# An edge-sorting graph kernel: the row numbers of its one-hots move to PSUM, its first steps and its plan are reordered

## What is computed

```
h        = relu(layernorm(x))                                   # x: 12500 x 256
in_deg   = min(segment_sum(1, dst), 511);  out_deg = min(segment_sum(1, src), 511)
sum3d    = segment_sum(edge_attr @ W_sum + b_sum, src)          # 212500 x 128 -> 12500 x 256
cent     = sigmoid(centralities @ W_cent + b_cent);  vor = sigmoid(voronoi @ W_vor + b_vor)
out      = x + h + z_in[in_deg] + z_out[out_deg] + cent + vor + sum3d
```

## Time and profile before

| what | value |
|---|---|
| times of three runs | 2588.72, 2579.75, 2586.4 us (median 2586.4) |
| the profiled execution's own time | 2585.49 us |
| its span in the profile | 2583.7 us |
| POOL busy | 1921.2 us, 74% of the span, 1869 instructions |
| DVE busy | 1754.8 us, 68% |
| PE busy | 1697.2 us, 66% |
| ACT busy | 764.1 us, 30% |
| DMA | 451.92 MB, 175 GB/s on average |

### The profile page before, as it was taken

One profiled execution on the slowest core, in us unless ns is written; L12 is line 12 of the kernel. 1 busy time (PEld: TensorE's weight loads), 2 busy tenths in 40 slices (PEclk: granted clock), 3 DMA queues, 4 the chain that ended last, 5 costly groups with the idle time before them and its releaser, 6 DMA issues. The chain is left out here.

```text
span 2583.7 us, 40662 instructions
## 1 busy us (share of the span) xinstructions
PE 1697.2 (66%) x8685; PEld 1207.0 (47%) x8685; DVE 1754.8 (68%) x5839; ACT 764.1 (30%) x3968; POOL 1921.2 (74%) x1869
## 2 busy tenths in 40 slices
PE   4755666655656565556877777674677785588766
PEld 1224444443334443334655555552565563476555
DVE  8764556778776587886766665552666674599776
ACT  1322222344442344444232323323233322001100
POOL 4877777777777777777777777777777777745787
PEclk7855665555556555557888888885889997899877
DMA  4336544445555443336776777774788785898975
GB/s 110 87 105 184 163 123 127 129 137 171 177 168 157 127 124 109 100 95 188 235 216 204 215 212 213 204 214 123 227 236 243 230 241 163 188 242 210 252 199 149
DMA packets 484919, 451.92 MB, mean 175 GB/s; under 512 B 72379, under 2 KB 444609, under 8 KB 484675
## 3 DMA queue, kind: packets, MB, share of 16 engines
q1 hardware_dynamic: 402782, 300.08, 43.3%
q0 software_dynamic: 78752, 136.44, 16.7%
q10 hardware_dynamic: 3140, 12.80, 1.5%
HBM read 319.28 MB, written 129.59 MB: 174 GB/s over the span
## 5 line engine op out<-in xcount | busy, mean ns | idle before, releaser
L476 POOL DMA_INDIRECT sorted<-edge_ring,pos_i x1660 | 1666.9, 1004 | 537.9 <-issue 483.5
L937 PE MATMUL bank<-piece_ring,hot_n 128*125 128x129 f32 x4920 | 901.0, 333 | 192.4 <-DVE hot_n L627 186.8
L937 PEld LDWEIGHTS bank<-piece_ring,hot_n 128*125 128x125 f32 x4920 | 776.6, 227 | 367.9 <-DVE hot_n L627 319.9
L627 DVE SCALAR_TENSOR_TENSOR hot_n<-bank,wkey,piece_ring 128x250 f32<-128x250 f32 x1230 | 576.7, 469 | 137.8 <-DMA piece_ring<-sorted 134.9
L825 ACT ACTIVATE junk<-bank,mark_col 128x100 bf16<-128x100 f32 x1664 | 548.5, 341 | 264.0 <-PE bank L921 263.4
L927 PE MATMUL bank<-hot_w,after_b 128*128 128x400 bf16 x416 | 183.1, 440 | 364.9 <-ACT junk L825 362.5
L832 ACT ACTIVATE edge_ring<-key_f 128x5 f32<-128x5 f32 x332 | 70.5, 212 | 1165.5 <-DMA edge_ring<-in_edge_attr_dram 1164.8
L961 PE MATMUL bank<-hot_dl,hot_dh 128*125 128x100 bf16 x1661 | 245.0, 303 | 235.4 <-DVE hot_dh L562 234.3
L652 DVE TENSOR_TENSOR acc<-bank,acc 125x129 f32 x1230 | 347.7, 283 | 51.1 <-PE bank L937 36.4
L763 DVE CAST pos_i<-pos_f 128x4 int32<-128x4 f32 x416 | 78.1, 188 | 444.9 <-ACT junk L825 441.0
L961 PEld LDWEIGHTS bank<-hot_dl,hot_dh 128*125 128x125 bf16 x1661 | 202.6, 207 | 310.9 <-DVE hot_dh L562 291.9
(11 more groups left out here) (99 smaller groups left out, 1081.4 us busy)
## 6 DMA issues: line engine op xcount, KB each, us to landing
piece_ring<-sorted SPq DMA_DIRECT2D x1230, 130.0 KB
edge_ring<-in_edge_attr_dram SPq DMA_DIRECT2D x332, 320.0 KB
sorted<-edge_ring,pos_i POOLq DMA_INDIRECT x1660
base<-in_x_dram SPq DMA_DIRECT2D x20, 560.0 KB
out_dram<-base ACTq DMA_DIRECT2D x20, 560.0 KB
out_dram<-base SPq DMA_DIRECT2D x9, 560.0 KB
base<-out_dram SPq DMA_DIRECT2D x9, 560.0 KB
edge_ring<-in_L_gnn_z_in_dram,deg_i POOLq DMA_INDIRECT x100, 6.6
```

What stands on the lines that cost most here:

```text
L476: g.indirect_dma_start(rows, bass.IndirectOffsetOnAxis(index, 0), edge_ring[:, slot, at, :], None).then_inc(s_scatter[slot], 16)
L627: v.scalar_tensor_tensor(out=hot_n[:, n % HOT_SLOTS, 0:G, :], in0=iota_ps.unsqueeze(1).to_broadcast([P, G, LOC]), scalar=wkey[:, s % 2, c: ...
L937: last = t_.matmul(to, hot_n[:, n % HOT_SLOTS, k, :], piece_ring[:, n % PIECE_SLOTS, k, 0:SUM], start=(k == 0), stop=(k == ROW_GROUPS[s] - 1))
```

## The change

- The row numbers for `hot_tiles` are now also in PSUM: `iota_h` is copied, as 125 f32 words, into a free part of bank 4 and read from there as bf16 pairs (`iota_pair`). All 1664 one-hots of the four kinds read them there instead of from SBUF.
- For the first two quads (`INDEX_FIRST`) `index(q)` stands ahead of the side work. The lists of segment 0 move from quad 0 to quad 8, the two further source key chunks from quads 0 and 1 to quads 3 and 6, and the totals of the next segment start ten quads into a segment instead of one.
- Segments are 40, 170, 125 and 81 quads. `HEAD` grows to 160 columns so that the first 40 quads have their keys from chunk 0. The pieces become 180, 440, 350 and 260.
- `acc` is zeroed by five ACT instructions over 2580 elements (a broadcast zero column) at quads 2, 6, 10, 14 and 18, instead of four DVE memsets. The first fold waits for all five.
- The planner's table of costs has other numbers, and its budget for a quad is 5.5 instead of 5.1.

```diff
-HEAD = 100
+HEAD = 160
-SEGMENT_QUADS = (25, 185, 125, 81)
+SEGMENT_QUADS = (40, 170, 125, 81)
+INDEX_FIRST = 2
-BUDGET = 5.1
+BUDGET = 5.5
-BASE = (0.7, 1.4, 2.5)
+BASE = (0.8, 1.4, 2.5)
...
-    CLEARS = 4
+    CLEARS = 5
...
-    put(0, ("lists", 0, 0))
+    put(8, ("lists", 0, 0))
     for i in range(CLEARS):
-        put(2 + 2 * i, ("clear", i, 0))
+        put(2 + 4 * i, ("clear", i, 0))
     for i in range(1, SRC_KEYS):
-        put(i - 1, ("keys", i, 0))
+        put(3 * i, ("keys", i, 0))
...
-        if left and q >= quad0[s] + 1:
+        if left and q >= quad0[s] + 10:
...
+        zero_col = sb("zero_col", [P, 1])
...
+        iota_pair = bank[4][:, P:P + LOC].bitcast(BF16).rearrange("p (n t) -> p n t", t=2)
...
             v.tensor_copy(iota_ps, iota_n[:, 0:LOC])
+            dve.wait_ge(s_made, 3)
+            link(v.tensor_copy(bank[4][:, P:P + LOC], iota_h[:, :, :].rearrange("p n t -> p (n t)").bitcast(F32)))
...
                 return v.tensor_tensor(to, part.unsqueeze(2).to_broadcast([P, 2, n, 2]),
-                                       iota_h[:, 0:n, :].unsqueeze(1).to_broadcast([P, 2, n, 2]), ALU.is_equal)
+                                       iota_pair[:, 0:n, :].unsqueeze(1).to_broadcast([P, 2, n, 2]), ALU.is_equal)
...
+                if n == 0:
+                    dve.wait_ge(s_acc_clear, CLEARS)
...
-            def clear(i):
-                n = SW // CLEARS
-                cleared[0] = mark(v.memset(acc[:, i * n:(i + 1) * n, :], 0.0))
...
                     hot_rows(q + 1)
+                if q < INDEX_FIRST:
+                    index(q)
...
-                index(q)
+                if q >= INDEX_FIRST:
+                    index(q)
...
+                    elif what == "clear":
+                        n = SW // CLEARS
+                        a.activation(acc[:, s * n:(s + 1) * n, :].rearrange("p w n -> p (w n)"),
+                                     zero_col[:, :].to_broadcast([P, n * SUM]), ACT.Copy).then_inc(s_acc_clear, 1)
```

More of the change, by code:

```diff
@@ L53 @@
 COUNTED = 2
-BUDGET = 5.1
+BUDGET = 5.5
 BACKLOG = 2.0
-BASE = (0.7, 1.4, 2.5)
-COST = {"keys": (8.0, 0.0, 0.0), "totals": (0.36, 0.4, 0.0), "starts": (2.0, 0.0, 0.0), "lists": (8.0, 2.0, 0.0),
-        "hist": (0.65, 1.1, 0.0), "stats": (0.62, 0.0, 0.0), "degrees": (2.0, 0.0, 0.0), "indegrees": (0.3, 0.0, 0.0),
-        "clear": (3.5, 0.0, 0.0), "node": (2.3, 0.0, 1.3), "piece2": (0.78, 0.75, 0.0)}
+BASE = (0.8, 1.4, 2.5)
+COST = {"keys": (8.0, 0.0, 0.0), "totals": (0.42, 0.43, 0.0), "starts": (2.0, 0.0, 0.0), "lists": (8.0, 2.0, 0.0),
+        "hist": (0.85, 1.1, 0.0), "stats": (0.62, 0.0, 0.0), "degrees": (2.0, 0.0, 0.0), "indegrees": (0.3, 0.0, 0.0),
+        "clear": (0.0, 0.0, 2.5), "node": (2.3, 0.0, 1.3), "piece2": (0.78, 0.75, 0.0)}
 def gnn_kernel(nc, x, src, dst, edge, cent, vor, z_in, z_out, w_cent, b_cent, w_vor, b_vor, w_sum, b_sum,
@@ L296, in gnn_kernel @@
         s_cleared = sem("s_cleared")
+        s_acc_clear = sem("s_acc_clear")
         s_keys = sem("s_keys")
@@ L518, in _ @@
             v.memset(mark_col[:, :], -MARK)
+            v.memset(zero_col[:, :], 0.0)
             v.memset(ones_b[:, :], 1.0).then_inc(s_cleared, 1)
@@ L646, in fold @@
                 dve.wait_ge(s_piece, n + 1)
-                if n == 0:
-                    need(cleared[0])
-                else:
+                if n > 0:
                     dve.wait_ge(s_summed, n)
@@ L652, in fold @@
                 v.tensor_tensor(to, ps_piece[n % PIECE_BANKS][0:LOC, 0:SUM], to, ALU.add).then_inc(s_summed, 1)
-            cleared = [0]
-            def clear(i):
-                n = SW // CLEARS
-                cleared[0] = mark(v.memset(acc[:, i * n:(i + 1) * n, :], 0.0))
             def hist(h):
@@ L765, in _ @@
             keys(0)
-            dve.wait_ge(s_made, 3)
             for h in range(quad0[1]):
@@ L789, in _ @@
                         degrees(s)
-                    elif what == "clear":
-                        clear(s)
                     elif what == "node":
```

## The result

The changed kernel takes 2523.5 us in the median (2522.8 to 2524.1, four runs) against 2587.6 us of the kernel before (2579.8 to 2589.3, four runs). The ratio is 0.976 with a 95% interval of 0.974 to 0.977. The prediction said 2524 us, with a range of its own of 2501 to 2550, and the measurement agrees. Its rivals A (2546), B (2642) and C (2568) did not come about.

What follows compares the result with a forecast made beforehand. POOL's chain of indirect-DMA scatters was taken to bound the kernel. Terms 5.4 + 2.0 + 11.0 + 43.5 = 61.9 us off the profiled 2585.5 gave 2523.6, with 0.9 to the median 2524 us, range 2501 to 2550.

Steps and rivals of the forecast that it cites:

- A: DVE's one-hots from PSUM run at the f32 rate, 170 us more DVE work, mostly absorbed: 2546 us; chance 0.12.
- B: PSUM one-hots at f32 rate and DVE's waits stay, POOL starves 118 us at quads 90 to 219: 2642 us; chance 0.07.
- C: Any DVE one-hot reading SBUF at the pair rate still holds POOL, so 43.5 us stay: 2568 us; chance 0.08.
- First scatter: POOL's start: quad 0's cast moves right behind the first one-hots, start at 27.9 us instead of 33.3, 5.4 us less.
- Second quad: POOL's wait of 2.31 us at 41.23 falls to 0.30, 2.0 us less, if the next quads come faster.
- One-hots: `hot_tiles` on DVE has one SBUF input, so scatters are held less: 43.5 us less, bounds 19.9 and 64.3.
- mean below 0.96 before 430 us: Sign of being right: POOL's scatters at line 476 have a mean duration below 0.96 us before 430 us.
- Memsets: Four memsets of 2746 ns leave DVE and no longer stretch POOL's scatters: 11.0 us less, bounds 9 to 13.
- DVE at the same rate: DVE instructions comparing with row numbers in PSUM keep 359 and 412 ns: cost taken as zero.
- What holds POOL: Some DVE instructions with two SBUF inputs stretch scatters, 1.24 us instead of 0.96; an input in PSUM seems the difference.
- Clears on ACT: Five zeroing instructions on ACT, 2.2 us each, at most 4.4, covered by keys and casts running ahead: cost nothing.
- Plan: Planner and segments spread the same instructions otherwise, no more or less POOL work: 0 us if DVE keeps ahead.

## Why the prediction was right, step by step

- **First scatter, 5.4 us**: measured 5.85 (33.26 to 27.41). The size of the added totals was right to half a microsecond.
- **Second quad, 2.0 us**: measured 2.01, the wait of 2.31 is the usual 0.30.
- **One-hots, 43.5 us**: the stretches say 11.3 us (165 to 430, predicted 13.3), 18.7 (430 to 1165, predicted 20.0) and 3.9 (1200 on, predicted 6.6). Taking the step back alone costs 47 us of time and 49.4 of durations, so it is a little larger than its term. By stretch it brings back 17.4 us of excess (19.4 less 2.0), 20.1 (38.5 less 18.4) and 8.8 (11.5 less 2.7): the split of the shared 37.1 us was right, and the stretches on either side of it were set too low. The sign "mean below 0.96 before 430 us" did not come: from 165 to 430 us it is 0.964 (201.57 / 209).
- **Memsets, 11.0 us**: the size was right and the cause was not. The first stretch lost 17.3 us of excess where 11.0 + 3.6 were predicted, and the four long scatters are gone, but ACT was not needed for it: with the memsets still on DVE, PSUM one-hots remove all four and the new order three. The step that failed is the sentence that charged the 3.4 us to the memset because it lay in the scatter; the instructions behind it were not looked at. That the sum came out in spite of it is luck: the three edits remove the same hold, and it was counted once.
- **DVE at the same rate, 0 us**: right, 354 and 406 ns. The rule of the Trainium skill that gave rivals A and B, one element a cycle for tensor_tensor with any operand in PSUM ("VectorE: DVE Perf Modes", "The perf-mode tier table"), does not hold for bf16 here. "At most two" ("Why PSUM operands drop a tier") fits both rates.
- **What holds POOL**: the earlier trace rows were read rightly. The page "SBUF — State Buffer" of the Trainium skill, section "SBUF: two separate sides", says that a DVE operation with two SBUF inputs, or in a two-port mode, and a GpSimd operation exclude each other for the whole instruction, in the first case only if the GpSimd operation reads SBUF. For the one-hots the runs agree that two SBUF inputs decide (1788.4 against 1608.7 us at equal rate). They add that most scatters beside such a one-hot lose nothing and a few lose nearly two microseconds to a run of them: 49.4 us over 1660 scatters. The holds of 3.69 and 4.20 us beside memsets stood with single-input instructions, so two SBUF inputs are not all that can hold POOL; no run tests the clause on two-port modes.
- **Clears on ACT, 0 us**: right. Each took 2.34 to 2.36 us, between the bounds of 2.2 and 4.4. The cast at 32.31 us is that of quad 2, whose positions stand ahead of the clear. Those of quad 3 end at 35.92, behind it, their cast starts at 39.05, behind the chunk of keys, and POOL starts on them at 43.60 after its usual 0.30 us: the keys and the cushion cover the clear, as predicted.
- **Plan, 0 us**: nothing in the profile speaks against it: POOL's waits on the cast are 35.5 us, of which 24.2 are the start, and the tail is unchanged. The old costs were tried only on a chip where POOL isn't the bound, so this stays without a test of its own. With the one-hots still in SBUF, the start order and the segments together gained 20 us where 7.4 and 0 had been put down for them; the scatters' durations gave 10.6 of it, the memsets among them.
- **The whole**: 61.9 us predicted for the profiled execution, 62.1 in the span. That it is this close is partly luck, since single stretches were off by up to 3 us in both directions and one term had the wrong cause.

## What to carry to other kernels

When one engine's chain of equal instructions sets the time, compare the mean duration of one with its least: the difference times the count is a price list of what disturbs it, and the stretches and instants in which it arises say which instruction of another engine to change. Here a constant operand of DVE in PSUM instead of SBUF freed GpSimd's indirect DMAs at no cost in rate, for bf16 and for f32 alike; what costs rate is a change from a 16-bit type to f32 (406 to 667 ns for 500 elements). Before a long neighbour is blamed for a stretched instruction, look at what stands behind that neighbour, and find one instance where it stands there and stretches nothing.

## What was not expected of the hardware

- A bf16 tensor_tensor with one input in PSUM runs at the rate of two SBUF inputs: 354 ns for 400 elements and 406 for 500, against 359 and 412. With f32 row numbers it takes 667 to 670 ns for 500 from either memory.
- Beside 60 of 66 memsets on DVE no scatter was held. In six cases a scatter beside one took 3.2 to 4.4 us and ended 1.0 to 1.3 us after the memset; each had a run of wide SBUF instructions behind it. The condition is not settled.
- With both inputs of the one-hots in SBUF, one scatter took 2.90 us beside eight one-hots and a cast, while 431 of the 722 that overlapped a one-hot took less than 1.0 us.
- On two chips the kernel before takes about 466 us longer. In the kernels profiled there POOL waits 410 to 641 us for DVE and ACT up to 1230 us for something unnamed, while the median scatter (0.96 us) and a one-hot from the bf16 pairs (353 and 407 ns) last as long as elsewhere. Edits that shorten the scatters, POOL's bound elsewhere, were worth nothing there.
